# A four-part neighbour search with last-layer units beside it, last layer mostly in whole units

## The chip, the cores and the metric

The kernel runs on one core of one Trainium2 chip. The metric is the device time of one execution in microseconds (us), median of the runs shown. The engines are TensorE (PE), VectorE (DVE), ScalarE (ACT), GpSimd (POOL) and SyncE (SP, which only issues DMAs here); they run independently and meet at semaphores.

## The reference

Four graph layers follow one another over 4096 nodes with 128 features, each with a residual. `adj` is 4096 x 4096 in fp32 and is used in all four:

```python
h = jnp.maximum(_layernorm(x), 0.0); x = x + _L0(h, adj)   # relu([h, adj@h] W + b)
h = jnp.maximum(_layernorm(x), 0.0); x = x + _L1(h, adj)   # normalised (adj+I) h, rows of unit length
h = jnp.maximum(_layernorm(x), 0.0); x = x + _L2(h, adj)   # message and GRU cell
h = jnp.maximum(_layernorm(x), 0.0); x = x + _L3(h, adj)
# _L3(x, A):
z  = leaky_relu(lap_mul(A, x) @ W1 + b1)                  # d * (A @ (d*x)), d = 1/sqrt(row sums of A)
d2 = sq[:, None] + sq[None, :] - 2.0 * (z @ z.T)          # 4096 x 4096 squared distances
S  = exp(-sqrt(max(d2, 0) + 1e-10) / 2)
S  = where(rank of S in its row < 4, S, 0)                # the four nearest nodes of each node
out = lap_mul(S + A, x) @ W2 + b2
```

So the last layer multiplies by `adj` twice: once to get `z`, and, after a search for the four nearest nodes of each row, once more with new row sums.

## The kernel before

`adj` does not fit on the core. It is streamed in units, and two layers share a load where both can use it. A *visit* is one unit of 128 x 2 x 512 numbers (512 KB) that PE multiplies; it is loaded by SP into one of 10 slots of a ring (`load_unit`), which has to wait until PE has used the unit ten visits back. A block is 512 nodes; a block's row of `adj` is 16 units (`UNITS`), numbered `u`, two for each block `kb` of columns. A class `Plan` writes down the order of all 524 visits, which PSUM bank each accumulation has, and after which visit each small step is due on each engine. Layers are numbered `q`; 4 stands for the second multiplication of the last layer.

A unit is multiplied in one of two ways (`visit` in the tensor block):

- *whole*: two fp32 products straight from the ring (the profile shows four matmuls, L441). No other engine is needed. The plan's own cost is 1.73 us (`WHOLE_US`).
- *split*: ACT copies the unit rounded to fp32r (`upper`, `A_hi`), DVE subtracts it from the original (`lower`, L1078, `A_lo`), and PE makes three fp32r products for each half (L436, L437, L438), six matmuls. The plan's cost is 1.38 us (`SPLIT_US`).

The first 396 visits are the first four multiplications. Then come three stages that the change touches.

**The last block and the start of the search.** When the last block of layer 3 is done, PE transposes it (`natural`), DVE makes `z`, PE transposes `z` (L551), ACT squares it, DVE makes the row of squares in three bf16 parts (`square_parts`), PE turns it into a row (`square_row`, L561), ACT writes it into `sq_aug` (`aug_out`).

**The search.** Nodes are taken 128 at a time (a row tile, 32 in all, in the order `seek`). For each, PE fills all eight PSUM banks with scores against all 4096 nodes, in two halves of four banks: four bf16 products with `ones3` (L611) and twelve fp32r products (L613 to L615) per half. ACT moves each half to one of two `scores` buffers (`pair_out`), 2048 columns at a time. DVE finds the eight largest of 4096 (`v_.max`, L1154) and their places (`v_.max_index`, L1156). A `scores` buffer is free when the scan two tiles back is finished. Every four tiles a short chain makes the similarities, the new row sums and the scaled operand of that block: `clamp` (DVE), `similarity` (ACT), `new_degrees` (DVE), `new_roots` (ACT), `new_inverse` (DVE), `scale_last` (ACT, gives `G_last` and its rounded copy), `last_rest` (DVE). POOL stores each scaled block to HBM (L1250). Because the scores have all eight banks, no last-layer visit can run before the last half is moved out.

**The last layer.** 128 visits: the 16 of block 0 whole, then blocks 1 to 7 with two whole units and 14 split ones each, in all 98 split. Beside it POOL gathers the four nearest rows of each node from HBM with indirect DMAs, 128 of them (L1258), once the last block is stored and all scans are done. There are eight landing slots; the gather for tile `t` waits until DVE has weighed tile `t - 8`. ACT scales the four rows (`scale_neighbours`), DVE adds them (`weigh`, L1189, L1191) and after every fourth tile finishes a block (`last_rows`, L1197 to L1205), which SP sends out. After which visit these are placed in the queues of ACT and DVE is set by `LAST_US`, `NEAR_US` and `NEAR_FIRST`:

```python
at = min(UNITS + int((NEAR_FIRST + NEAR_US * t) / LAST_US), UNITS * NB)
self.near_due.setdefault(self.rows_end + at, []).append(t)
```

All queues are in order: a step that waits on ACT holds the `upper` behind it, and so DVE's `lower` and PE.

Of the kernel before, what the change touches and what calls it, by code (L numbers as in the profile page):

```python
# [5 lines left out]
P = 128  # L6
N = 4096
BLK = 512
# [54 lines left out]
WHOLE_BESIDE_SCANS = tuple(range(UNITS))  # L63
WHOLE_LAST = (7, 15)

LAST_US, NEAR_US, NEAR_FIRST = 1.5, 6.1, 9.0


class Plan:


    def __init__(self):
# [25 lines left out]
        for n in range(UNITS * NB):  # L100
            b, j = n // UNITS, n % UNITS
            u = j if b else (NB - 1 - j // HALVES) * HALVES + j % HALVES
            self.visits.append(Visit(len(self.visits), b, u, (4,), j not in (WHOLE_BESIDE_SCANS, WHOLE_LAST)[b > 0]))
            self.spans.setdefault((4, b, 4), [len(self.visits) - 1, 0])[1] = len(self.visits) - 1
# [4 lines left out]
        for t in range(NT):  # L109
            at = min(UNITS + int((NEAR_FIRST + NEAR_US * t) / LAST_US), UNITS * NB)  # L110
            self.near_due.setdefault(self.rows_end + at, []).append(t)
# [12 lines left out]
        for b in range(NB):  # L124
            self.moved["move_out", 4, b] = len(self.moved) + 1

# [74 lines left out]
def gnn_stack(nc, x_in, at_in, pack_in, scaled_rows, out):  # L201
# [4 lines left out]
    with ctx:  # L206
# [18 lines left out]
        a_at, b_at, hi_at = take("area_a", 16), take("area_b", 16), take("area_hi", 4 * STAGED)  # L225

# [23 lines left out]
        colsum = sb("colsum", [P, TPB, BLK])  # L250
# [17 lines left out]
        sq_aug = colsum[0:3, :, :].bitcast(bf16).rearrange("p t (b n) -> p (t b) n", n=BLK)  # L268
        sq_cols = sb("sq_cols", [P, TPB])
        sq_parts = sb("sq_parts", [P, TPB, 3], bf16)  # L270
        sq_rest = sb("sq_rest", [P, 2, TPB])
        ident16 = sb("ident16", [P, P], bf16)
        ones3 = sb("ones3", [3, P], bf16)
# [40 lines left out]
        half_full, half_out, scanned = sem("half_full"), sem("half_out"), sem("scanned")  # L314
# [23 lines left out]

        first_hn = (hn, nat)
# [6 lines left out]
        def _(sp):  # L346
# [15 lines left out]
            sent = 0  # L362
# [9 lines left out]
            for v in PLAN.visits[SLOTS:]:  # L372
                load_unit(v)
                for t in PLAN.near_due.get(v.n - SLOTS - 2, ()):
                    if t % TPB == TPB - 1:
                        send(t // TPB)
                        sent += 1
            for b in range(sent, NB):
                send(b)
# [4 lines left out]
        def _(pe):  # L384
# [17 lines left out]
            def operand_of(v, q, p):  # L402

                kb = v.u // HALVES
                if q == 0 and v.split:
                    pe.wait_ge(firstlo_ready, NB)
                elif q == 0:
                    pe.wait_ge(first_ready, kb + 1)
                elif q < 4:
                    pe.wait_ge(g_ready, nth_h(q - 1, kb) - NB)  # L410
                elif v.b == 0:
                    pe.wait_ge(lastlo_ready if v.split else last_ready, NB - kb)
                else:
                    pe.wait_ge(lastlo_ready, NB)
# [139 lines left out]
            def square_row(b):  # L554
# [5 lines left out]
                for n in range(TPB):  # L560
                    last = mm(ps[0:3, GB, n * P:(n + 1) * P], sq_parts[:, n, :], ident16[:, :], start=True, stop=True)  # L561
# [38 lines left out]


            half_of = lambda c: (c // 4 + 1) % 2
            columns = (*range(4, 8), *range(4))
            bank_of = lambda c: c % 4 + 4 * half_of(c)

            def pair_columns(t, cs):

                at_row = t % TPB * P
                hi, lo = (z[:, t // TPB, at_row:at_row + P] for z in (z_hi, z_lo))
                for c in cs:  # L610
                    mm(ps[:, bank_of(c), :], ones3[:, :], sq_aug[:, c, :], start=True, stop=False)  # L611
                for c in cs:
                    mm(ps[:, bank_of(c), :], hi, z_hi[:, c, :], start=False, stop=False)  # L613
                    mm(ps[:, bank_of(c), :], hi, z_lo[:, c, :], start=False, stop=False)  # L614
                    last = mm(ps[:, bank_of(c), :], lo, z_hi[:, c, :], start=False, stop=True)  # L615
                last.then_inc(half_full, 1)

            def pair_rows(i):
                for half in range(2):
                    pe.wait_ge(half_out, 2 * i + half - 1)  # L620
                    pair_columns(seek[i], columns[4 * half:4 * half + 4])

            def first_pairs(cs):

                for c in cs:
                    pe.wait_ge(aug_ready, nth_in(3, c))
                    pe.wait_ge(zlo_ready, nth_in(3, c))
                pair_columns(seek[0], cs)
# [4 lines left out]
            first_pairs(columns[0:4])  # L633
# [5 lines left out]
            pe.wait_ge(half_out, 2 * NT)  # L639

            for v in PLAN.visits[PLAN.rows_end:]:
                visit(v)
                if v.b and v.u == 2 + (v.b == 1):
# [5 lines left out]
        def _(act):  # L649
# [107 lines left out]
            def aug_out(b):  # L757
                act.wait_ge(sqrow_full, nth_in(3, b))
                f(sq_aug[:, b, :], ps[0:3, GB, :], ACT.Copy).then_inc(aug_ready, 1)
# [74 lines left out]
            def pair_out(i):  # L834
# [3 lines left out]
                for half in range(2):  # L838
                    act.wait_ge(half_full, 2 * i + half + 1)
                    at_col = N // 2 * (1 - half)  # L840
                    f(scores[i % 2][:, at_col:at_col + N // 2],
                      ps[:, 4 * half:4 * half + 4, :].rearrange("p c n -> p (c n)"), ACT.Identity,
                      scale=2.0, bias=neg_sq[:, t:t + 1]).then_inc(half_out, 1)
# [50 lines left out]
            for j, v in enumerate(PLAN.visits[PLAN.rows_end:]):  # L894
                if v.split:
                    upper(v)
                if v.b and j % UNITS == 3:
# [4 lines left out]
            for t in PLAN.near_due.get(PLAN.rows_end + UNITS * NB, ()):  # L902
# [4 lines left out]
        def _(dve):  # L907
# [148 lines left out]
            def square_parts(b):  # L1056
# [6 lines left out]
                half, rest = sq_rest[:, 0, :], sq_rest[:, 1, :]  # L1063
                own.add(v_.tensor_scalar(half, sq_cols[:, :], -0.5, None, ALU.mult))
                own.settle()
                own.add(v_.tensor_copy(sq_parts[:, :, 0], half))
                own.settle()
                own.add(v_.tensor_tensor(rest, half, sq_parts[:, :, 0], ALU.subtract))
                own.settle()
                own.add(v_.tensor_copy(sq_parts[:, :, 1], rest))  # L1070
                own.settle()
                v_.tensor_tensor(sq_parts[:, :, 2], rest, sq_parts[:, :, 1], ALU.subtract).then_inc(sqparts_ready, 1)
# [57 lines left out]
            v_.tensor_copy(ident16[:, :], ident)  # L1130
# [17 lines left out]

            def scan(i):

                t = seek[i]
                dve.wait_ge(half_out, 2 * i + 2)
                row = scores[i % 2][:, :]
                own.add(v_.max(best[:, t, :], row))  # L1154
                own.settle()
                v_.max_index(best_at[:, t, :], best[:, t, :], row).then_inc(scanned, 1)  # L1156
# [50 lines left out]
            for i in range(NT - 2):  # L1207
# [7 lines left out]
                elif i >= TPB:  # L1215
                    last_rest(i // TPB - 1)
            m = NB - 1
# [79 lines left out]
```

## Time and profile before

| | |
|---|---|
| median of 3 runs | 1424.39 us (1424.10 to 1429.17) |
| the profiled execution | 1424.92 us, span in the trace 1423.1 us |
| PE busy | 93% of the span (modelled ends) |
| DVE busy | 84% |
| ACT busy | 56% |
| POOL busy | 12% |
| read from HBM | 286 MB |
| mean granted TensorE clock | 0.977 |

The span is what the trace covers; the device time has 1.8 us more. Times in the text are positions on the trace's own clock, which starts with the span. Busy PE time overlaps itself, as each matmul's end is modelled; the pace of PE is read from the starts of successive matmuls.

### The profile page before, as it was taken

How to read it: one execution, taken by the hardware profiler on the slowest of the kernel's cores; microseconds unless marked ns; L12 is line 12 of the kernel's file. 1: busy time of each engine (PE TensorE's matmuls, PEld its weight loads, DVE VectorE, ACT ScalarE, POOL GpSimd, SP SyncE). 2: the span in 40 equal slices, each digit the busy share in tenths (PEclk: the TensorE clock that was granted, in tenths of full speed). 3: DMA queues.
4: the chain of work that ended last, by engine and by line, in shares of the span. 5: the costliest groups of instructions: out<-in, count | busy, mean ns of one | idle time of the engine just before them, and what ended most of it. 6: DMA issues, size and time to landing. Idle time of an engine off the chain costs nothing.

```text
span 1423.1 us, 15737 instructions
## 1 busy us (share of the span) xinstructions
PE 1321.7 (93%) x5526; PEld 955.9 (67%) x5526; DVE 1191.1 (84%) x1616; ACT 790.9 (56%) x1117; POOL 173.0 (12%) x144
## 2 busy tenths in 40 slices
PE   7999999999899999999999999899989989899983
PEld 4556677788778767777777778555555554677662
DVE  8998889898999878766548998599999998587784
ACT  2423333346766767665557776455555554676773
POOL 0000000000000000000000000000000000888885
PEclk9999999999999999999999999999999999999997
DMA  9787766558676866565558799100000005989993
GB/s 348 230 268 245 223 209 203 181 188 308 235 243 225 280 245 225 181 220 194 179 176 295 264 329 343 55 0 8 8 8 8 8 8 186 371 314 367 377 337 101
DMA packets 82861, 291.49 MB, mean 205 GB/s; under 512 B 10848, under 2 KB 10976, under 8 KB 82784
## 3 DMA queue, kind: packets, MB, share of 16 engines
q1 hardware_dynamic: 78048, 280.01, 56.8%
q0 software_dynamic: 4736, 10.49, 2.5%
q8 instruction: 44, 0.72, 0.2%
q14 instruction: 33, 0.27, 0.1%
HBM read 286.27 MB, written 4.19 MB: 204 GB/s over the span
## 4 chain that ended last, share of the span: by engine, by line
PE 50%; DVE 29%; POOL 12%; issue 6%; ACT 2%; DMA 1%; SPq 0%; POOLq 0%; ACTq 0%; DVEq 0%
POOL landing L1258 12%; PE ps L436 11%; PE ps L438 11%; PE ps L437 11%; DVE best_at L1156 9%; DVE rows_T L1154 9%; PE ps L441 7%; DVE A_lo L1078 6%; PE ps L511 1%; PE ps L539 1%; PE ps L540 1%; PE ps L480 1%; PE ps L474 1%; DVE hn L928 1%; PE ps L498 1%
## 5 line engine op out<-in xcount | busy, mean ns | idle before, releaser
L1078 DVE TENSOR_TENSOR A_lo<-ring,A_hi 128x1024 fp32r<-128x1024 f32 x431 | 508.9, 1219 | 61.7 <-ACT A_hi L651 58.1
L651 ACT ACTIVATE A_hi<-ring 128x1024 fp32r<-128x1024 f32 x431 | 440.0, 1054 | 110.0 <-PE ps L438 98.1
L436 PE MATMUL ps<-A_hi,G_odd_hi 128*128 128x512 f32 x708 | 291.2, 411 | 17.0 <-DVE A_lo L1078 10.1
L438 PE MATMUL ps<-A_hi,G_odd_lo 128*128 128x512 f32 x708 | 280.4, 396 | 0.0
L437 PE MATMUL ps<-A_lo,G_odd_hi 128*128 128x512 f32 x708 | 280.2, 396 | 0.0
L1258 POOL DMA_INDIRECT landing<-scaled_rows,best_at x128 | 166.3, 1299 | 43.4 <-issue 38.7
L436 PEld LDWEIGHTS ps<-A_hi,G_odd_hi 128*128 128x128 f32 x708 | 135.3, 191 | 52.1 <-issue 18.6
L436 PE MATMUL ps<-A_hi,G_even_hi 128*128 128x512 f32 x386 | 162.5, 421 | 0.2 <-DVE A_lo L1078 0.2
L651 ACT ACTIVATE scores<-ps,neg_sq 128x2048 f32<-128x2048 f32 x64 | 124.3, 1963 | 59.9 <-PE ps L615 38.3
L437 PEld LDWEIGHTS ps<-A_lo,G_odd_hi 128*128 128x128 f32 x708 | 135.6, 192 | 29.9 <-issue 3.4
L438 PEld LDWEIGHTS ps<-A_hi,G_odd_lo 128*128 128x128 f32 x708 | 135.6, 192 | 29.8
L1250 POOL DMA_DIRECT2D scaled_rows<-G_last x8 | 6.2, 780 | 1197.5 <-ACT G_last L651 1197.5
L438 PE MATMUL ps<-A_hi,G_even_lo 128*128 128x512 f32 x386 | 150.7, 390 | 0.0
L437 PE MATMUL ps<-A_lo,G_even_hi 128*128 128x512 f32 x386 | 150.4, 390 | 0.0
L1154 DVE MAX8 rows_T<-scores 128x8 f32<-128x4096 f32 x32 | 141.3, 4414 | 9.6 <-ACT scores L651 9.6
L1156 DVE FIND_INDEX8 best_at<-rows_T,scores 128x8 uint32<-128x4096 f32 x32 | 141.4, 4419 | 0.0
L958 DVE TENSOR_TENSOR colsum<-colsum,ring 128x1024 f32<-128x1024 f32 x112 | 133.7, 1219 | 0.0
L441 PE MATMUL ps<-ring,G_first 128*128 128x512 f32 x252 | 113.2, 592 | 0.0
L613 PE MATMUL ps<-z_hi 128*128 128x512 f32 x256 | 110.9, 433 | 0.0
L614 PE MATMUL ps<-z_lo,z_hi 128*128 128x512 f32 x256 | 103.7, 405 | 0.0
L615 PE MATMUL ps<-z_hi,z_lo 128*128 128x512 f32 x256 | 103.7, 405 | 0.0
L611 PE MATMUL ps<-colsum,ones 3*128 3x512 bf16 x256 | 66.9, 380 | 26.8 <-ACT scores L651 26.1
(136 smaller groups left out, 1354.8 us busy)
## 6 DMA issues: line engine op xcount, KB each, us to landing
ring<-adj_t SPq DMA_DIRECT2D x524, 512.0 KB
X<-x_rows SPq DMA_DIRECT2D x8, 256.0 KB, 6.9
scaled_rows<-G_last POOLq DMA_DIRECT2D x8, 256.0 KB, 2.7
landing<-scaled_rows,best_at POOLq DMA_INDIRECT x128
out_rows<-X SPq DMA_DIRECT2D x8, 256.0 KB
pack<-packed SPq DMA_DIRECT2D x1, 836.0 KB, 14.6
pack<-packed SPq DMA_DIRECT2D x1, 192.0 KB, 4.1
```

The source lines that it names most:

```text
L436: mm(acc, G_hi[odd][:, kb, t, :], hi, start=start, stop=False)
L437: mm(acc, G_hi[odd][:, kb, t, :], lo, start=False, stop=False)
L438: done = mm(acc, G_lo[odd][:, kb, t, :], hi, start=False, stop=stop)
L441: done = mm(acc, G[:, kb, t, :], ring[:, s, k, :], start=start, stop=stop)
L613: mm(ps[:, bank_of(c), :], hi, z_hi[:, c, :], start=False, stop=False)
L614: mm(ps[:, bank_of(c), :], hi, z_lo[:, c, :], start=False, stop=False)
L651: return nc.scalar.activation(out_ap, in_ap, func, **k)
L958: ins = v_.tensor_tensor(half, half, ring[:, s, :, :], ALU.add)
L1078: v_.tensor_tensor(A_lo[:, s, :, :], ring[:, s, :, :], A_hi[:, slot_of(v), :, :].bitcast(fp32), ALU.subtract).then_inc(lower_ready, 1)
L1154: own.add(v_.max(best[:, t, :], row))
L1156: v_.max_index(best_at[:, t, :], best[:, t, :], row).then_inc(scanned, 1)
L1258: pool.indirect_dma_start(out=landing[:, k, r, :], out_offset=None, in_=scaled_rows, in_offset=bass.IndirectOffsetOnAxis(ap=best_at[:, t, ...
```

## The change

It does the following.

- `square_parts` makes two fp32r parts in place of three bf16 ones; `square_row` multiplies them in fp32; `sq_aug` is 128 rows deep, cleared once by POOL, and has its own place together with `colsum`. `ones2` replaces `ones3`.
- The search is done in four parts of two banks (`columns`, `pair_columns`, `score_banks`), which rotate through three pairs of banks. Two banks are left. ACT moves 1024 columns at a time (`evicted` counts them).
- 34 last-layer visits are placed into PE's stream before the end of the search: one after each of 17 row tiles from the 9th to the 30th (three tiles in four), and 17 behind the last row tile (11 of blocks 0 and 1, six of block 2). All are whole.
- The remaining 94 visits are whole but for units 4 and 12 of each block (11 visits).
- At the end of the search DVE does both last `max` scans before the first `max_index`, with `clamp` and `new_degrees` between.
- `near_due` counts from the end of the search with 5.2 us for a tile in place of 6.1; SP sends the finished blocks after all loads.

```diff
-WHOLE_BESIDE_SCANS = tuple(range(UNITS))
-WHOLE_LAST = (7, 15)
-LAST_US, NEAR_US, NEAR_FIRST = 1.5, 6.1, 9.0
+LAST_US, NEAR_US, NEAR_FIRST = 1.7, 5.2, 8.0
+SPLIT_EVERY = 8
...
-        for n in range(UNITS * NB):
-            b, j = n // UNITS, n % UNITS
-            u = j if b else (NB - 1 - j // HALVES) * HALVES + j % HALVES
-            self.visits.append(Visit(len(self.visits), b, u, (4,), j not in (WHOLE_BESIDE_SCANS, WHOLE_LAST)[b > 0]))
+        ended = [b * HALVES + half for b in sorted(range(NB), key=lambda b: self.rank[3, b]) for half in range(HALVES)]
+        self.beside = {}
+        for c in range(28):
+            v = self.last_visit(c % 2, ended[c // 2], False)
+            at = 8 + c // 3 * 4 + c % 3
+            self.beside.setdefault(at if at < NT - 2 else NT - 1, []).append(v)
+        for u in ended[:6]:
+            self.beside[NT - 1].append(self.last_visit(2, u, False))
+        self.search_end = len(self.visits)
+        for b in range(2):
+            for u in ended[-HALVES:]:
+                self.last_visit(b, u, False)
+        for b in range(2, NB):
+            for u in range(UNITS):
+                if b > 2 or u not in ended[:6]:
+                    self.last_visit(b, u, u % SPLIT_EVERY == SPLIT_EVERY // 2)
...
+            at = self.search_end + int((NEAR_FIRST + NEAR_US * t) / LAST_US)
+            if t % TPB == TPB - 1:
+                at = max(at, self.search_end + 13, self.spans[4, t // TPB, 4][1] + 8)
+            self.near_due.setdefault(min(at, len(self.visits)), []).append(t)
...
+        columns = [sorted(seek_blocks[2 * q:2 * q + 2]) for q in range(4)]
+        free = [k for k in range(2 * BANKS) if k not in (PLAN.bank[4, 0, 4], PLAN.bank[4, 1, 4])]
+        score_banks = (free[0:2], (AUX, AUX + 1), (TB, GB))
...
+            def pair_columns(i, q):
+                n, at_row = 4 * i + q, seek[i] % TPB * P
+                if n >= len(score_banks):
+                    pe.wait_ge(evicted, n - len(score_banks) + 1)
+                hi, lo = (z[:, seek[i] // TPB, at_row:at_row + P] for z in (z_hi, z_lo))
+                for bank, c in zip(score_banks[n % len(score_banks)], columns[q]):
+                    mm(ps[:, bank, :], ones2[:, :], sq_aug[:, c, :], start=True, stop=False)
+                    mm(ps[:, bank, :], hi, z_hi[:, c, :], start=False, stop=False)
+                    mm(ps[:, bank, :], hi, z_lo[:, c, :], start=False, stop=False)
+                    last = mm(ps[:, bank, :], lo, z_hi[:, c, :], start=False, stop=True)
+                last.then_inc(part_full, 1)
...
+            first_columns(0)
             z_transposes(last_row)
+            first_columns(1)
             square_row(last_row)
-            first_pairs(columns[4:8])
+            first_columns(2)
+            first_columns(3)
             for i in range(1, NT):
-                pair_rows(i)
+                for q in range(4):
+                    pair_columns(i, q)
+                for v in PLAN.beside.get(i, ()):
+                    if v.b == 2:
+                        pe.wait_ge(evicted, 4 * NT)
+                    visit(v)
...
-            scan(NT - 2)
+            scan_values(NT - 2)
+            scan_values(NT - 1)
+            clamp(m)
+            scan_places(NT - 2)
+            new_degrees(m)
+            scan_places(NT - 1)
+            new_inverse(m)
             last_rest(m - 1)
-            scan(NT - 1)
-            clamp(m)
-            new_degrees(m)
-            new_inverse(m)
             last_rest(m)
...
+            pool.wait_ge(u_ready, NB)
+            pool.wait_ge(nat_full, 3 * NB)
+            g.memset(sq_aug[:, :, :].bitcast(fp32), 0.0).then_inc(aug_cleared, 1)
```

## Rows read from the trace of the kernel before

**Rows 1.** The page's costliest groups: line, engine, operation; busy and mean; idle and its releaser.

```profile
L1258 POOL DMA_INDIRECT landing<-scaled_rows,best_at x128 | 166.3, 1299 | 43.4 <-issue 38.7
...
L1154 DVE MAX8 rows_T<-scores 128x8 f32<-128x4096 f32 x32 | 141.3, 4414 | 9.6 <-ACT scores L651 9.6
```

**Rows 2.** Table by stage: window, length, busy of PE, PEld, DVE, ACT, POOL; PEclk, DMA share, GB/s.

```profile
908.00:1181.00 273.00, 246.88 (x976) 155.94 (x975) 271.67 (x125) 150.07 (x127) 4.74 (x6) 0.97 0.02 6
1185.00:1213.00 28.00, 27.54 (x65) 12.27 (x65) 19.58 (x14) 11.30 (x20) 4.50 (x5) 1.00 0.79 274
...
1290.00:1320.00 30.00, 28.04 (x108) 20.63 (x106) 23.17 (x32) 20.89 (x34) 24.82 (x18) 0.94 0.99 363
```

**Rows 3.** Timeline of POOL: start us, us, engine, line; gathers of the last layer.

```profile
1209.38 1.47 POOL L1258 DMA_INDIRECT landing<-scaled_rows,best_at  x1 [4.65 <-DMA scaled_rows<-G_last]
...
1233.41 0.94 POOL L1258 DMA_INDIRECT landing<-scaled_rows,best_at  x1 [0.31 <-issue]
...
1246.01 1.97 POOL L1258 DMA_INDIRECT landing<-scaled_rows,best_at  x1 [0.30 <-issue]
...
1395.52 0.95 POOL L1258 DMA_INDIRECT landing<-scaled_rows,best_at  x1 [0.30 <-issue]
...
1413.42 0.94 POOL L1258 DMA_INDIRECT landing<-scaled_rows,best_at  x1 [0.30 <-issue]
```

**Rows 4.** Timeline of DVE around two of those gathers.

```profile
1228.80 4.63 DVE L1078 TENSOR_TENSOR A_lo<-ring,A_hi 128x1024 fp32r<-128x1024 f32 x4 [0.20 <-issue]
...
1244.80 4.63 DVE L1078 TENSOR_TENSOR A_lo<-ring,A_hi 128x1024 fp32r<-128x1024 f32 x4
```

**Rows 5.** Timeline of PE in the search: the halves of one row tile.

```profile
1175.52 1.03 PE L611 MATMUL ps<-colsum,ones 3*128 3x512 bf16 x4
...
1176.82 0.40 PE L614 MATMUL ps<-z_lo,z_hi 128*128 128x512 f32 x1
...
1178.88 0.39 PE L614 MATMUL ps<-z_lo,z_hi 128*128 128x512 f32 x1
...
1179.43 1.03 PE L611 MATMUL ps<-colsum,ones 3*128 3x512 bf16 x4
```

**Rows 6.** Timeline of PE: the 16 whole units of block 0, then split units.

```profile
1185.46 27.73 PE L441 MATMUL ps<-ring,G_last 128*128 128x512 f32 x64 [2.06 <-ACT scores L651]
1212.63 0.79 PE L436 MATMUL ps<-A_hi,G_odd_hi 128*128 128x512 f32 x1
```

**Rows 7.** Timeline of ACT and DVE at the start of the search.

```profile
906.07 1.97 ACT L651 ACTIVATE scores<-ps,neg_sq 128x2048 f32<-128x2048 f32 x1 [4.47 <-PE ps L615]
...
908.07 4.43 DVE L1154 MAX8 rows_T<-scores 128x8 f32<-128x4096 f32 x1 [9.58 <-ACT scores L651]
```

**Rows 8.** Timelines at the end of the search: the last two scans, the last store.

```profile
1180.33 4.40 DVE L1154 MAX8 rows_T<-scores 128x8 f32<-128x4096 f32 x1
...
1194.29 4.42 DVE L1156 FIND_INDEX8 best_at<-rows_T,scores 128x8 uint32<-128x4096 f32 x1
...
1202.20 0.18 DVE L1175 RECIPROCAL d2inv<-root 128x4 f32<-128x4 f32 x1 [1.15 <-ACT root L651]
...
1203.98 0.75 POOL L1250 DMA_DIRECT2D scaled_rows<-G_last  x1 [16.37 <-ACT G_last L651]
```

**Rows 9.** Two lines asked for by source: their first and last start (us).

```profile
L1035 DVE TENSOR_TENSOR colsum<-colsum x8: 692/693/694, 521.8 to 754.3; 128x512 f32<-128x512 f32 x8
...
L561 PE MATMUL ps<-ident,sq_parts x32: 217/219/311, 789.3 to 898.8; 128*3 128x128 bf16 x32
```

**Rows 10.** Timeline of ACT and DVE at the end of the kernel.

```profile
1400.76 0.60 ACT L651 ACTIVATE rows_T<-ps 128x512 f32<-128x512 f32 x1 [6.44 <-issue]
1401.25 2.44 ACT L651 ACTIVATE landing<-landing,simil 128x128 f32<-128x128 f32 x8
...
1416.00 1.27 ACT L651 ACTIVATE landing<-landing,simil 128x128 f32<-128x128 f32 x4 [3.66 <-DMA landing<-scaled_rows,best_at]
...
1419.99 0.69 DVE L1205 TENSOR_TENSOR X<-X,nat 128x512 f32<-128x512 f32 x1
```

More of the change, by code:

```diff
@@ L360, in send @@
                 sp.dma_start(out[b, :, :, :], X[:, b, :, :]).then_inc(out_stored, 16)
-            sent = 0
             load_x(0)
@@ L373, in _ @@
                 load_unit(v)
[L374 to L378, printed above, removed]
+            for b in range(NB):
                 send(b)
@@ L599, in _, with first_columns @@
                         step(name, p, b)
[L602 to L628, printed above, removed]
+            def pair_columns(i, q):
[9 more added lines that the diff above has]
+                last.then_inc(part_full, 1)
+            def first_columns(q):
+                done = NB if q > 1 else max(nth_in(3, c) for c in columns[q])
+                pe.wait_ge(aug_ready, done)
+                pe.wait_ge(zlo_ready, done)
+                pair_columns(0, q)
             last_row = seek_blocks[-1]
@@ L837, in pair_out @@
                     act.wait_ge(scanned, i - 1)
[L838 to L843, printed above, removed]
+                for q in range(4):
+                    act.wait_ge(part_full, 4 * i + q + 1)
+                    (bank, next_bank), at_col = score_banks[(4 * i + q) % len(score_banks)], columns[q][0] * BLK
+                    f(scores[i % 2][:, at_col:at_col + 2 * BLK], ps[:, bank:next_bank + 1:next_bank - bank, :].rearrange("p c n -> p (c n)"),
+                      ACT.Identity, scale=2.0, bias=neg_sq[:, t:t + 1]).then_inc(evicted, 1)
             def similarity(m):
@@ L893, in _ @@
             scale_last(m)
-            for j, v in enumerate(PLAN.visits[PLAN.rows_end:]):
+            for v in PLAN.visits[PLAN.search_end:]:
                 if v.split:
                     upper(v)
-                if v.b and j % UNITS == 3:
+                if v.n - PLAN.search_end in (6, 10):
+                    move_out(4, (v.n - PLAN.search_end) // 4 - 1)
+                elif v.b > 2 and v.u == 3:
                     move_out(4, v.b - 1)
@@ L901, in _ @@
             move_out(4, NB - 1)
-            for t in PLAN.near_due.get(PLAN.rows_end + UNITS * NB, ()):
+            for t in PLAN.near_due.get(len(PLAN.visits), ()):
                 scale_neighbours(t)
@@ L1147, in _, with scan_values, scan_places @@
                     step(name, p, b)
-            def scan(i):
[L1151 to L1156, printed above, removed]
+            def scan_values(i):
+                dve.wait_ge(evicted, 4 * i + 4)
+                own.add(v_.max(best[:, seek[i], :], scores[i % 2][:, :]))
+            def scan_places(i):
+                own.settle()
+                v_.max_index(best_at[:, seek[i], :], best[:, seek[i], :], scores[i % 2][:, :]).then_inc(scanned, 1)
+            def scan(i):
+                scan_values(i)
+                scan_places(i)
             def clamp(m):
@@ L1231, in _ @@
                         last_rows(t // TPB)
-            for t in PLAN.near_due.get(PLAN.rows_end + UNITS * NB, ()):
+            for t in PLAN.near_due.get(len(PLAN.visits), ()):
                 weigh(t)
```

59 lines of the change are left out of this document (28 added, 31 removed).

## Prediction

> **What bounds the kernel now.** I read the page first, then the table by stage, then the timeline of each engine around the places that the change touches. In the search DVE is the bound: 271.7 of 273 us busy, PE's clock at 0.97, DMA at a share of 0.02 [rows 2]. The first `max` starts at 908.07 [rows 7] and the last `max_index` ends at 1194.29 + 4.42 = 1198.7 [rows 8]: 290.6 us for 32 row tiles, 9.08 each. PE needs 3.91 us for a half [rows 5], 7.8 of the 9.08, and is not used otherwise; the loads stand still.
>
> In the last layer the order turns. Gathers run from 1209.38 to 1413.42, and their idle time is all "issue": POOL never waits for a landing slot [rows 1, 3]. So POOL is busy from end to end, 204.0 us for 127 steps, 1.607 each. PE is done earlier: ACT moves out the last block at 1400.76, and what comes later is the last gathers and their tail [rows 10]. DMA is close to full beside it (share 0.99 at 363 GB/s [rows 2]). Two limits thus lie close together: POOL sets the end, and PE could not end much earlier, since it starts this layer only when the last scores are moved out.
>
> **Why a gather takes 0.94 or 1.97 us.** The one at 1233.41 begins just as a run of `lower` ends (1228.80 + 4.63) and takes 0.94; the one at 1246.01 lies inside the run from 1244.80 to 1249.43 and takes 1.97 [rows 3, 4]. From 1395.52, after the last `lower`, 15 gathers start 17.90/14 = 1.279 us apart [rows 3]. The first 113 steps take 186.1 us, 1.647 each: 41.6 us more than at 1.279, or 0.42 us for each of the 98 split units. The Trainium skill ("SBUF — State Buffer", Who interferes with whom) says that a DVE instruction with two SBUF inputs contends with a GpSimd instruction that reads SBUF; by that, the trace agrees. The same section infers that `tensor_tensor` would not hold up descriptor generation; by that alone gathers would stay as they are, which is the first rival below.
>
> **Before the search.** `square_parts` loses three DVE instructions of some 0.2 us per block; `square_row` goes from bf16 to fp32, four matmuls of 128 columns. A whole unit's fp32 matmul has 512 columns and takes a quarter of 1.70 us (below), so 128 columns cost about 0.1 and the four at most 0.5 us, beside 0.2 now. Over eight blocks that is between -5 and +3 us on engines that have other work beside; I take 0. POOL's clearing of `sq_aug` (4096 elements a row) can start when the last GRU block is made (last L1035 at 754.3) and a transpose later; the first `square_row` is at 789.3 [rows 9]. It has some 30 us. DVE reads 4096 elements in 4.4 us [rows 1]; POOL may take several times that, still hidden. At ten times, ACT would wait about 15 us with `upper` behind it, part of which DVE and the ring could not give back. I take 0.
>
> At the start of the search PE now puts 8 matmuls, not 16, ahead of the transposes of the last `z`: 8 at 0.229 us (2.06 us for nine [rows 5]), 1.8 us. Three small DVE steps less: 0.6. The last move-out before the first scan is of 1024 columns, not 2048: half of 1.97, so 1.0 [rows 7]. Sum -3.4 us (bounds 0, if PE's second 8 matmuls take the place of the first, and -4.5). The first scan starts at 904.7.
>
> **The search.** DVE's work per tile is unchanged, so 9.08 stands if PE keeps up. A tile is 32 matmuls of 0.229, `ones2` priced like its fp32r neighbours: 7.33 us. Whole units: 16 took 1212.63 - 1185.46 = 27.17 us, 1.70 each, and the next matmul 0.4 more for the change of type [rows 6]. Beside scores I take 1.75, at most 2.1. Three visits in four tiles: (4 x 7.33 + 3 x 1.75)/4 = 8.64 us of 9.08, at the clock of 0.97 8.91, and at 2.1 still 8.9 before the clock. A tile's scores are due a whole scan after their buffer is free, and four move-outs of 1.0 us and a part of 1.8 us need under 6 us, so a late part has 3 us of slack. I take 0; at most the missing 0.2 us x 22 tiles, 4 us. All of DVE's other work stays. So 17 units of 1.7 us disappear under the scans.
>
> **The end of the search.** The last buffer is free at 1180.33 - 3.4 = 1176.9 [rows 8]. The first move-out frees a pair at 1177.9, PE's last part is done at 1179.8. From there it goes on without waiting: 17 whole units, 28.9 us, to 1208.7. The block scaled last is needed only behind them.
>
> DVE does max, max, index, index, the same 18.4 us, to 1195.3; but `clamp` and `new_degrees` lie inside, and `new_inverse` follows at once, where it came 3.5 us after the scan (1202.20 against 1198.7). The store came 1.8 us after it, the first gather 5.4 us later [rows 3, 8]: now 1197.2 and 1202.6, 6.8 us earlier than before.
>
> **The last layer on PE.** 83 whole units at 1.70, 141.1; 11 split at the plan's 1.38, 15.2; seven transposed blocks at 0.7 (estimate, under the 1.03 of four matmuls in [rows 5]), 4.9. From 1208.7 to 1369.9. The clock: 1.00 over the whole units, 0.94 in a later window [rows 2]. Two such windows of 30 us cost 3.4 us; none and all are 0 and 11. I take 3.4: 1373.3. Before, PE had this work spread up to 1400.6, with 32 us less in price but 17 units more to do and the loads and `lower` to wait for.
>
> **The gathers.** 127 x 1.279 + 11 x 0.42 = 167.0 us after 1202.6: the last starts at 1369.6. Before, ACT took it up 2.58 us later [rows 3, 10]: 1372.2. The last `scale_neighbours` stand behind the last `move_out` in ACT's queue, so PE's end decides by some 3 us. If only the gathers counted, the end would be 1369.6 + 9.7 (1423.1 - 1413.42) = 1379.3.
>
> **The tail.** ACT starts 0.15 after PE, the scalings 0.49 later and take 2.44; from the end of the last scaling (1417.27) to the end of the span it was 5.8 [rows 10]. 1373.3 + 3.1 + 5.8 = 1382.2. Sending all blocks after the loads costs nothing: seven of them go while the ring is already loaded.
>
> **The loads.** From 1177 on 101 units of 0.524 MB and 128 gathers of 0.066 MB are 61.4 MB. At PE's pace this is 308 + 50 = 358 GB/s against 363 seen [rows 2], tight, but ten slots give 17 us of slack; DMA decides only under 61.4/196 = 313 GB/s on the mean.
>
> Waits added in queues: `scale_neighbours(t)` waits on ACT before an `upper`. Gather t is landed at about 1202.6 + 5.3(t + 1) + 2.5, the visit behind it due at 1208.7 + 1.7(8 + 5.2t)/1.7: ACT is 8 us ahead at t = 0, and about 5 at t = 27, before the last split unit. No hold. Sum: span 1382.2; the profiled execution had 1.8 us beside its span (1424.9 against 1423.1) and is 0.5 us from the median, so 1384.
>
> **Rivals.**
> - *The gathers do not get faster.* If the load of the DMA engines, not `lower`, makes them long, the step stays 1.607: 1202.6 + 204.1 + 9.7 = 1416.4, and 1418 with the 1.8. That is -0.45%, no change that can be told. For it: DMA is idle too after 1395. Against: the 0.94 at 1233.41. Chance 0.06.
> - *They get half as fast as I say,* since `weigh` and `last_rows`, now bunched, or the loads lengthen them too: 1.45 gives 1202.6 + 184.2 + 9.7 + 1.8 = 1398, and ACT then holds the uppers. 0.10.
> - *DMA is the bound,* 330 GB/s beside the gathers: 1.87 us a unit, 16 us more less some slack: 1393 to 1400. 0.05.
> - *The clock falls (slower).* PE is now busy 95% of the search and all of the last layer, and nothing covers it. With clock c it costs 22 (8.64/c - 9.08) + 190 (1/c - 1) us. At 0.885 this eats the 40 us won; at 0.85 the time is about 1438. Against: 0.97 to 1.00 in all windows with PE at work but the last ones at 0.94 [rows 2]. 0.04.
> - *My sum,* 1376 to 1392: 0.75.
>
> **Numbers.** 1384, range 1376 to 1402, which holds the sum and the two middle rivals; low end by no clock loss (-3.4) and -4 before the search. 0.5% (7 us) is about what a measurement tells from no change. Faster 0.90, same 0.06, slower 0.04.
>
> **What would show it.** Gathers start near 1203 and 1.3 us apart, 0.94 but beside `lower`; first scan near 905 and 9.1 us a tile, with DVE never waiting for scores; PE starts whole units near 1180, 1.70 us apart, to about 1373; POOL ends a few us before. Wrong if DVE waits for ACT's scores, if gathers last over 1.2 us with DVE idle, if PE waits for the ring, or if PEclk is under 0.95.

## The result, and the profile after

| | before | after |
|---|---|---|
| median | 1424.64 us (1424.10 to 1429.17, 4 runs) | 1380.76 us (1379.87 to 1382.12, 4 runs) |
| profiled execution, its span | 1424.92, 1423.1 | 1379.87, 1378.0 |
| PE, DVE, ACT, POOL busy | 93, 84, 56, 12% | 96, 79, 52, 10% |
| mean granted clock | 0.977 | 0.996 |

The ratio is 0.9686 with a 95% interval of 0.9664 to 0.9708: 44 us, 3.1%, less. 1384 was forecast, with 1376 to 1402 as the range.

Two of the page's costliest groups, after, against [rows 1]. The scan's `max` takes what it took; the 128 gathers take 990 ns on the mean where they took 1299.

```profile
L1167 DVE MAX8 rows_T<-scores 128x8 f32<-128x4096 f32 x32 | 141.3, 4415 | 7.4 <-ACT scores L672 7.4
...
L1287 POOL DMA_INDIRECT landing<-scaled_rows,best_at x128 | 126.7, 990 | 43.5 <-issue 38.1
```

The table by stage, after (columns as in [rows 2]): the search, the stretch from its last scores to the first gathers, and the rest of the last layer.

```profile
900.00:1176.00 276.00, 261.85 (x1057) 198.75 (x1056) 271.34 (x125) 164.15 (x189) 4.75 (x6) 0.99 0.12 39
1180.00:1209.00 29.00, 29.00 (x69) 12.93 (x68) 15.04 (x12) 7.43 (x16) 7.29 (x9) 1.00 0.85 292
1209.00:1370.00 161.00, 160.31 (x426) 77.84 (x425) 52.74 (x113) 53.48 (x140) 120.95 (x122) 1.00 0.95 344
```

In the search DVE is as full as it was, and DMA is no longer idle. Behind it PE is busy 160.3 of 161 us at a clock of 1.00; from 1290 to 1320 us the kernel before had 0.94 [rows 2].

The timeline of POOL, after, against [rows 3, 8]: the last store, the first gather, two from the middle, the last.

```profile
1195.86 0.75 POOL L1279 DMA_DIRECT2D scaled_rows<-G_last  x1 [13.21 <-ACT G_last L672]
...
1201.38 1.02 POOL L1287 DMA_INDIRECT landing<-scaled_rows,best_at  x1 [4.78 <-DMA scaled_rows<-G_last]
...
1235.50 1.22 POOL L1287 DMA_INDIRECT landing<-scaled_rows,best_at  x1 [0.30 <-issue]
...
1245.85 1.57 POOL L1287 DMA_INDIRECT landing<-scaled_rows,best_at  x1 [0.31 <-issue]
...
1365.91 0.94 POOL L1287 DMA_INDIRECT landing<-scaled_rows,best_at  x1 [0.30 <-issue]
```

127 steps in 164.5 us are 1.296 each, against 1.607.

The timeline of DVE, after, against [rows 7, 8]: the first scan, and the last `max` and `max_index`.

```profile
903.39 4.43 DVE L1167 MAX8 rows_T<-scores 128x8 f32<-128x4096 f32 x1 [6.96 <-ACT scores L672]
...
1180.47 4.43 DVE L1167 MAX8 rows_T<-scores 128x8 f32<-128x4096 f32 x1 [0.41 <-ACT scores L672]
...
1189.76 4.42 DVE L1171 FIND_INDEX8 best_at<-rows_T,scores 128x8 uint32<-128x4096 f32 x1
```

The scans last from 903.39 to 1194.18, 9.09 us a tile. DVE waited for scores twice: before the first scan, and 0.41 us before the last `max`.

The timeline of PE, after, against [rows 5, 6]: one last-layer visit beside the scores, and the 19 whole visits that follow the last scores without a gap.

```profile
1042.43 1.88 PE L462 MATMUL ps<-ring,G_last 128*128 128x512 f32 x4
1043.74 0.79 PE L630 MATMUL ps<-sq_aug,ones 128*128 128x512 f32 x1
...
1179.55 32.78 PE L462 MATMUL ps<-ring,G_last 128*128 128x512 f32 x76
```

The end of the kernel, after, against [rows 10], on ACT:

```profile
1369.28 0.60 ACT L672 ACTIVATE rows_T<-ps 128x512 f32<-128x512 f32 x1 [6.80 <-PE ps L462]
1369.77 2.43 ACT L672 ACTIVATE landing<-landing,simil 128x128 f32<-128x128 f32 x8
```

Before, ACT had moved out the last block at 1400.76 and got the last gather's rows at 1416.00. Now the last gather starts at 1365.91, and 3.4 us later ACT takes PE's last block, and behind it the last two tiles' scalings with no wait for rows. By the 2.58 us of before, these rows were there at 1368.5, 1.3 us before ACT came to them: PE sets the end, with POOL close behind it. The span is 45.1 us shorter: the last move-out comes 31.5 us earlier, and what follows it takes 8.8 us in place of 22.4, since no gather is awaited there any more.

### The profile page after: what moved, and what is told of

Same layout as the page of the kernel before. It is cut to its first block, busy times and chain, and to the rows that moved or that the text cites. A ratio compares the mean times of both kernels' runs of the same rounds, so it can differ in the third digit from the quotient of the medians.

```text
span 1378.0 us, 15241 instructions
## 1 busy us (share of the span) xinstructions
PE 1325.3 (96%) x5384; PEld 949.2 (69%) x5384; DVE 1089.8 (79%) x1504; ACT 721.2 (52%) x1094; POOL 137.2 (10%) x146
## 4 chain that ended last, share of the span: by engine, by line
PE 66%; DVE 29%; ACT 2%; issue 2%; DMA 1%; SPq 0%; ACTq 0%; DVEq 0%
PE ps L462 19%; PE ps L457 12%; PE ps L459 12%; PE ps L458 12%; DVE best_at L1171 9%; DVE rows_T L1167 9%; DVE A_lo L1095 5%; PE ps L532 1%; PE ps L560 1%; PE ps L561 1%; PE ps L495 1%; PE ps L501 1%; DVE hn L951 1%; PE ps L519 1%; DVE stats L936 1%
## 5 line engine op out<-in xcount | busy, mean ns | idle before, releaser
L1095 DVE TENSOR_TENSOR A_lo<-ring,A_hi 128x1024 fp32r<-128x1024 f32 x344 | 409.6, 1220 | 64.9 <-ACT A_hi L672 62.6
L672 ACT ACTIVATE A_hi<-ring 128x1024 fp32r<-128x1024 f32 x344 | 354.8, 1056 | 106.3 <-PE ps L459 92.2
L457 PE MATMUL ps<-A_hi,G_odd_hi 128*128 128x512 f32 x534 | 217.8, 408 | 2.1 <-DVE A_lo L1095 2.1
L459 PE MATMUL ps<-A_hi,G_odd_lo 128*128 128x512 f32 x534 | 209.1, 392 | 0.0
L458 PE MATMUL ps<-A_lo,G_odd_hi 128*128 128x512 f32 x534 | 208.4, 390 | 0.0
L462 PE MATMUL ps<-ring,G_last 128*128 128x512 f32 x468 | 205.7, 592 | 0.0
L672 ACT ACTIVATE scores<-ps,neg_sq 128x1024 f32<-128x1024 f32 x128 | 137.4, 1111 | 51.3 <-PE ps L633 39.5
L462 PEld LDWEIGHTS ps<-ring,G_last 128*128 128x128 f32 x468 | 88.4, 190 | 99.4 <-issue 97.5
L1287 POOL DMA_INDIRECT landing<-scaled_rows,best_at x128 | 126.7, 990 | 43.5 <-issue 38.1
L630 PE MATMUL ps<-sq_aug,ones 128*128 128x512 f32 x256 | 109.0, 426 | 14.8 <-ACT scores L672 14.1
L458 PEld LDWEIGHTS ps<-A_lo,G_odd_hi 128*128 128x128 f32 x534 | 100.7, 189 | 22.4 <-issue 3.1
```

The lines of the kernel that those rows point to most:

```text
L457: mm(acc, G_hi[odd][:, kb, t, :], hi, start=start, stop=False)
L458: mm(acc, G_hi[odd][:, kb, t, :], lo, start=False, stop=False)
L459: done = mm(acc, G_lo[odd][:, kb, t, :], hi, start=False, stop=stop)
L462: done = mm(acc, G[:, kb, t, :], ring[:, s, k, :], start=start, stop=stop)
L630: mm(ps[:, bank, :], ones2[:, :], sq_aug[:, c, :], start=True, stop=False)
L672: return nc.scalar.activation(out_ap, in_ap, func, **k)
```

## The experiments

The kernels ran in groups, each on one chip together with the kernel before, and their ratios are against it there. The changed kernel, unaltered, was in two of the groups. In the one with the order of scans and the two with a visit after every row tile it took 1379.98 us (1378.48 to 1382.19), ratio 0.9678 [0.9660, 0.9696]. In the one with the split, behind and paced kernels it took 1379.96 (1379.19 to 1380.55), 0.9681 [0.9663, 0.9698]. The kernel before with a whole last layer ran on another chip, without the changed kernel beside it. The "stretch" of which some expectations speak is told under "Three runs with a stretch of their own".

> The changed kernel unaltered, timed beside the next three: 1381 us.

> The changed kernel unaltered, beside a repetition of three edits whose traces had a stretch of some 30 to 40 us from about 1233 in which PE issued one matmul in 2 to 3 us, ACT and DVE stood, SP issued hardly a load and only POOL's gathers went on. If that stretch belongs to the chip those three shared, this kernel has it too whenever the three have it, and none has it elsewhere (1381 us here); if it belongs to their programs, they have it here and this one doesn't.

### Most of the last layer split again

```diff
-                    self.last_visit(b, u, u % SPLIT_EVERY == SPLIT_EVERY // 2)
+                    self.last_visit(b, u, u % SPLIT_EVERY != SPLIT_EVERY - 1)
```

> 14 of 16 last-layer units split again. Without the stretch: DVE's subtractions lengthen the gathers again, the last starts near 1397, time 1409 us; PE alone as the bound would give 1377. With the stretch: 1403 to 1417 again.

Measured: 1404.63 us (1402.73 to 1407.15), ratio 0.9856 [0.9837, 0.9875]; 24.7 us more than the changed kernel beside it. The gathers of this kernel, by source (shortest, median and longest ns; first and last start):

```profile
L1287 POOL DMA_INDIRECT landing<-scaled_rows,best_at x128: 940/948/1982, 1202.1 to 1393.3; - x128
```

The step is 191.2/127 = 1.506 us, and (1.506 - 1.296) x 127 / 68 = 0.39 us more for each split unit, against the 0.42 read from the trace of before. The timelines of POOL and DVE show the mechanism, around 1233 and around 1299 us:

```profile
1233.38 1.55 POOL L1287 DMA_INDIRECT landing<-scaled_rows,best_at  x1 [0.30 <-issue]
1235.23 1.97 POOL L1287 DMA_INDIRECT landing<-scaled_rows,best_at  x1 [0.30 <-issue]
...
1298.19 0.94 POOL L1287 DMA_INDIRECT landing<-scaled_rows,best_at  x1 [0.30 <-issue]
1299.44 1.98 POOL L1287 DMA_INDIRECT landing<-scaled_rows,best_at  x1 [0.30 <-issue]
```

```profile
1232.90 3.49 DVE L1095 TENSOR_TENSOR A_lo<-ring,A_hi 128x1024 fp32r<-128x1024 f32 x3
...
1298.24 3.60 DVE L1095 TENSOR_TENSOR A_lo<-ring,A_hi 128x1024 fp32r<-128x1024 f32 x3 [0.20 <-ACT A_hi L672]
```

It is not any overlap that counts, but a `lower` that is running when the gather starts. The gather at 1298.19 starts 0.05 us before the first `lower` of the run and takes 0.94, though it lies beside it; the one at 1299.44 starts with the second one running and takes 1.98. In this trace 39 gathers start while a `lower` is running that has at least 0.2 us to go, and every one takes what that `lower` has left plus 0.82 us: 1.55 with 0.74 to go, 1.97 with 1.15. The 52 such gathers of the kernel before and the nine of the changed one do the same; over all hundred it is 0.81 to 0.83 us. So the gather is held until the `lower` has ended. Nine gathers of the split version start within 0.01 us of a `lower` or up to 0.4 us ahead of one, with no other DVE instruction running, and take 0.94 or 0.95. ACT's `upper`, which comes with every split unit too, is not the cause: 26 gathers lie beside an `upper` and no `lower`, with a median of 0.94 and none above 1.07.

The Trainium skill ("SBUF — State Buffer", Who interferes with whom) infers that `tensor_tensor` would not hold up descriptor generation. By that alone the gathers would stay as they are, and the trace does not agree: 1.97 against 0.94 us, and the step grows with the number of `lower`. Whether the descriptors or POOL's reading of the indices is held up, no trace here tells.

PE has 68 x 0.32 = 22 us less priced work in this kernel and still waits. Its waits from 1205 us on:

```profile
PE ps L457 <- DVE A_lo L1095: 32.0, 12, 4.8
PE ps L495 <- ACT rows_T L672: 0.7, 1, 0.7
```

These waits go back to the gathers as well. Eleven of the 12 are longer than 0.5 us, and ahead of ten of these the last thing that ACT waited for before the `upper` was the landing of gathered rows; then this `upper` was late, then DVE's `lower`, then PE. So the time does not show PE's work, and both limits end together: PE's last block is moved out at 1393.88, and ACT then waits 0.23 us for the rows of the last gather:

```profile
1395.88 1.28 ACT L672 ACTIVATE landing<-landing,simil 128x128 f32<-128x128 f32 x4 [0.23 <-DMA landing<-scaled_rows,best_at]
```

### The kernel before with a whole last layer

This leaves the search, its eight banks and the start of the last layer as before. Which units are split, and the pace of 5.2 us a tile, are the changed kernel's; the first step stays at 9.0 us, where the changed kernel has 8.0. The running maximum in the edit keeps the near steps (the scaling and weighing of a tile's four rows) in the order of the tiles.

```diff
-            ... j not in (WHOLE_BESIDE_SCANS, WHOLE_LAST)[b > 0]))
+            ... b > 0 and j % 8 == 4))
-LAST_US, NEAR_US, NEAR_FIRST = 1.5, 6.1, 9.0
+LAST_US, NEAR_US, NEAR_FIRST = 1.7, 5.2, 9.0
...
+        at = 0
         for t in range(NT):
-            at = min(UNITS + int((NEAR_FIRST + NEAR_US * t) / LAST_US), UNITS * NB)
+            at = max(at, UNITS + int((NEAR_FIRST + NEAR_US * t) / LAST_US))
+            if t % TPB == TPB - 1:
+                at = max(at, self.spans[4, t // TPB, 4][1] - self.rows_end + 8)
+            at = min(at, UNITS * NB)
```

> The kernel before, with its search as it was, but the last layer in whole units but two of each block (14 split), and the gathers' steps placed as in the changed kernel. Theory: the gathers are short (127 x 1.28 + 14 x 0.42 = 168 us, last start near 1378), and PE sets the end: 1212.6 + 98 x 1.70 + 14 x 1.38 + 4.9 = 1403.4, and 8.9 us of tail and 1.8 beside the span make 1414 us, so only a quarter of the whole gain. Rival (whole units alone bring the gain, the search in four parts little): about 1381 to 1390 us.

Measured: 1415.04 us (1414.69 to 1416.85), ratio 0.9939 [0.9920, 0.9958]. The gathers, by source:

```profile
L1262 POOL DMA_INDIRECT landing<-scaled_rows,best_at x128: 940/944/1995, 1209.9 to 1377.6; - x128
```

The gathers alone lose 36 us of their end (1413.4 to 1377.6), and the kernel gains 10: PE, now some 28 us behind them, transposes its last block at 1406.4. Cheaper gathers do not pay unless PE's work gets shorter too.

### All 34 early visits behind the search

```diff
-            self.beside.setdefault(at if at < NT - 2 else NT - 1, []).append(v)
+            self.beside.setdefault(NT - 1, []).append(v)
```

> The 17 visits between the row tiles behind the search again. Without the stretch: PE has 28.9 us more to do behind the search and the time is 1410 us. With it: 1443 us or more again.

Measured: 1409.68 us (1407.49 to 1410.92), ratio 0.9887 [0.9869, 0.9905]; 29.7 us more than the changed kernel, for 17 visits, against 17 x 1.70 = 28.9. The last gather starts at 1368.5, as good as unmoved, and PE's last block is transposed at 1400.3. In the search the window by engines reads:

```profile
900.00:1170.00 270.00, 238.56 (x970) 188.17 (x970) 263.85 (x121) 162.45 (x187) 4.75 (x6) 0.96 0.02 6
```

The scans take as long with the visits (9.09 us a tile) as without them.

### The old pace of the near steps

```diff
-LAST_US, NEAR_US, NEAR_FIRST = 1.7, 5.2, 8.0
+LAST_US, NEAR_US, NEAR_FIRST = 1.7, 6.1, 9.0
```

> The gathers' steps placed 6.1 us a tile apart again. If the stretch belongs to the chip of the first look: 1387 us, for five tiles more that are scaled and weighed after PE's end, and no such stretch. If it belongs to the program: 1425 us or more again.

Measured: 1386.32 us (1386.11 to 1387.34), ratio 0.9726 [0.9709, 0.9744]; 6.4 us more than the changed kernel beside it. Its timeline of ACT at the end:

```profile
1370.31 0.60 ACT L672 ACTIVATE rows_T<-ps 128x512 f32<-128x512 f32 x1 [14.93 <-PE ps L462]
1370.81 8.27 ACT L672 ACTIVATE landing<-landing,simil 128x128 f32<-128x128 f32 x28
```

The last block is moved out 0.5 us later than in the changed kernel beside it (1369.85). But 28 scalings, seven tiles, are placed behind it in ACT's queue where the changed kernel has eight: 8.27 against 2.43 us. ACT was idle for 14.93 us just before, though the rows of the first of these tiles had landed. The last gather starts 4.2 us later too (1370.33 against 1366.15), though POOL waited for no slot; its rows, landed near 1372.9, are not awaited, as ACT's scalings last to 1379.1. Here the pace costs on the tail.

### The old order of the last two scans

```diff
-            scan_values(NT - 2)
-            scan_values(NT - 1)
-            clamp(m)
-            scan_places(NT - 2)
-            new_degrees(m)
-            scan_places(NT - 1)
-            new_inverse(m)
-            last_rest(m - 1)
-            last_rest(m)
+            scan(NT - 2)
+            last_rest(m - 1)
+            scan(NT - 1)
+            clamp(m)
+            new_degrees(m)
+            new_inverse(m)
+            last_rest(m)
```

> The changed kernel with the two last scans in the old order (max, places, max, places, and clamp and new_degrees only behind them). Theory: the last store and the gathers come 3.5 us later (first near 1204.9, last near 1369.4); ACT could take up the last tile at 1372.0, where it did so at 1370.9, so the time grows by only 1 us, to 1382. Rival (the gathers set the end one for one): 1384.5.

Measured: 1380.72 us (1379.62 to 1383.48), ratio 0.9678 [0.9662, 0.9694], the same as the changed kernel's beside it. The timeline of POOL, the last store, the first gather and the last:

```profile
1199.83 0.75 POOL L1277 DMA_DIRECT2D scaled_rows<-G_last  x1 [16.69 <-ACT G_last L672]
...
1205.29 1.02 POOL L1285 DMA_INDIRECT landing<-scaled_rows,best_at  x1 [4.71 <-DMA scaled_rows<-G_last]
...
1372.08 0.94 POOL L1285 DMA_INDIRECT landing<-scaled_rows,best_at  x1 [0.30 <-issue]
```

The store and the first gather come 3.9 and 4.0 us later than in the changed kernel beside it (1195.96 and 1201.32), about the 3.5 of the theory: this is what the new order gives to the gathers. The profiled execution was the slowest of the five, 1383.48 us. In it the gathers also take longer, 1.313 us a step, the last one starts at 1372.08 and not at 1369.4, and ACT waits 1.24 us for its rows behind the last block. So the old order uses up POOL's slack, and in that execution more than that; on the median of five the end does not move by more than can be told.

### A visit after every row tile, 22 in place of 17

```diff
-            at = 8 + c // 3 * 4 + c % 3
+            at = 8 + c
```

> The changed kernel with a visit after every row tile from the 9th to the 30th, 22 in place of 17. PE then needs 7.43 + 1.72 = 9.15 us a tile against 9.08 of DVE. Theory: the search grows by no more than 2 us, PE ends 8.5 - 2 us earlier, and now the gathers set the end, about 2.4 us earlier than now at most: 1378 to 1380. Rival (PE, with no slack, makes the scans wait for scores by more than it saves): 1383 or more.

Measured: 1379.89 us (1379.32 to 1381.97), ratio 0.9676 [0.9660, 0.9693]: no gain, though the scans did not get longer. The timelines of PE and then ACT of this kernel from 1211 to 1221 us show where it went.

```profile
1211.42 2.31 PE L462 MATMUL ps<-ring,G_last 128*128 128x512 f32 x5
1220.00 0.77 PE L457 MATMUL ps<-A_hi,G_odd_hi 128*128 128x512 f32 x1 [6.26 <-DVE A_lo L1095]
1220.56 0.63 PE L458 MATMUL ps<-A_lo,G_odd_hi 128*128 128x512 f32 x1
1220.99 0.63 PE L459 MATMUL ps<-A_hi,G_odd_lo 128*128 128x512 f32 x1
```

```profile
1212.62 0.57 ACT L672 ACTIVATE rows_T<-ps 128x512 f32<-128x512 f32 x1
1216.37 1.28 ACT L672 ACTIVATE landing<-landing,simil 128x128 f32<-128x128 f32 x4 [3.17 <-DMA landing<-scaled_rows,best_at]
1217.55 1.04 ACT L672 ACTIVATE A_hi<-ring 128x1024 fp32r<-128x1024 f32 x1
```

PE comes to its first split unit earlier, but the `upper` of this unit stands in ACT's queue behind the scalings of a tile whose gathers have not landed. PE idles 6.26 us, and then runs for a while at the lower clock level: its matmuls start 0.43 us apart instead of 0.23. Its last block is moved out at 1369.33, as in the changed kernel (1369.28). The gathers would have left little more: the last starts at 1366.9, and with the 9.7 us from there to the end of the span and the 1.8 beside it, as in the kernel before, that is an estimate of 1378.4.

### The same, and no unit split

```diff
-            at = 8 + c // 3 * 4 + c % 3
+            at = 8 + c
...
-                    self.last_visit(b, u, u % SPLIT_EVERY == SPLIT_EVERY // 2)
+                    self.last_visit(b, u, False)
```

> As the one with a visit after every row tile, and no split unit in the last layer. Theory: PE +3.5 us for 11 units more in whole form, the gathers -11 x 0.42 = -4.6 us; both limits then lie near 1371 to 1374 on the trace: 1375 to 1377. Rival: the gathers are at their floor already (1.25 us each wherever the split units go), nothing gained over the 1378 to 1380 of the other.

Measured: 1375.84 us (1375.04 to 1378.12), ratio 0.9650 [0.9633, 0.9667], the best of the versions: 4.1 us less than the changed kernel beside it, and the two ranges do not meet. Its gathers:

```profile
L1287 POOL DMA_INDIRECT landing<-scaled_rows,best_at x128: 940/945/1405, 1201.8 to 1362.6; - x128
```

The step is 160.8/127 = 1.266, and PE waits for no `A_lo` any more. The longest gathers, up to 1.41 us without any `lower`, start beside other DVE additions of two SBUF tiles; one of `weigh`, as POOL and then DVE show it:

```profile
1252.29 1.19 POOL L1287 DMA_INDIRECT landing<-scaled_rows,best_at  x1 [0.30 <-issue]
```

```profile
1252.23 0.42 DVE L1208 TENSOR_TENSOR landing<-landing 128x256 f32<-128x256 f32 x1 [1.07 <-ACT landing L672]
```

Over the 128 gathers this comes to some 2 us (160.8 against 127 x 1.25). Five visits more hidden are 8.5 us, 11 units whole instead of split cost 11 x 0.32 = 3.5 us: 5.0 by the prices. PE sets the end, and the last gather starts 2.4 us before the last move-out (1362.56 and 1364.97).

### Three runs with a stretch of their own

The split, behind and paced kernels had first run on another chip, the same programs, with these results: 1415.71 us (1403.40 to 1416.94), 1449.00 (1442.99 to 1453.21) and 1429.55 (1424.70 to 1439.10), ratios 0.9894 [0.9842, 0.9946], 1.0156 [1.0113, 1.0199] and 1.0033 [1.0011, 1.0055].

> The changed kernel with 14 of 16 last-layer units split as before (79 split visits behind the search in place of 11). Theory (DVE's subtractions lengthen the gathers, about 0.42 us for each split unit): the gathers take 127 x 1.28 + 79 x 0.42 = 196 us from about 1201.4, the last starts near 1397, POOL sets the end again, and the time is 1409 us; gathers of 1.97 us come back. Rival (the gathers became short because the loads are spread otherwise, and PE is what counts): PE's work falls from 162 to 140 us, the gathers stay at 1.30 us, and the time is about 1377 us. Also open: PE's granted clock fell to 0.94 in windows of the kernel before's last layer and was 1.00 in the changed one's; if the split units are the cause, windows at 0.94 come back here.

> The changed kernel, but the 17 visits that stood between row tiles now stand behind the last row tile with the other 17. Theory (the visits between the scans cost nothing there, and PE sets the end): PE has 17 x 1.70 = 28.9 us more to do behind the search, everything else stays, 1410 us. Rival (the visits slow the scans, or DMA traffic beside them does): the first scan to the last takes less than the 290 us of the changed kernel, and the time is some us under 1410.

> The changed kernel with the gathers' steps placed 6.1 us a tile apart and 9.0 from the start, as before, in place of 5.2 and 8.0. Theory: the gathers themselves don't change (POOL finds its slot free), but seven tiles in place of two are scaled and weighed behind PE's last move-out, five times 1.25 us on ACT: 1387 us. Rival 1: no difference (1381), because the end hangs on PE alone. Rival 2: POOL waits for slots and the last gather starts 5 us or more later, 1392 us or more.

They were 11, 39 and 43 us over what the same programs took on the second chip. The traces of all three have one stretch in which most of the core stands, beginning between 1224 and 1235 us and lasting from some 22 us (behind) to some 45 (split). It is not in every execution: of the split kernel's four, one took 1403.40 us, what it took on the second chip. For the paced kernel, the window and two of its waits (the releaser is given as "remote"):

```profile
1230.00:1260.00 30.00, 12.38 (x20) 3.93 (x18) 0.00 (x0) 0.00 (x0) 22.66 (x24) 0.63 0.31 90
```

```profile
ACT rows_T L672 <- remote: 43.5, 1, 43.5
DVE nat L1216 <- remote: 32.7, 1, 32.7
```

PE's matmuls start 2.8 us apart, DVE and ACT do nothing, DMA moves 90 GB/s, and POOL's gathers go on as always, 24 in 30 us. (In the other two DVE and ACT do a little, and POOL pauses too.) The changed kernel on the second chip has in the same window:

```profile
1230.00:1260.00 30.00, 30.00 (x83) 14.78 (x82) 10.00 (x22) 10.26 (x27) 22.99 (x24) 1.00 0.99 353
```

The kernel before, on the first chip, took its usual 1426.81 us (1421.48 to 1428.61). The changed kernel itself was not run there. So the stretch depends on the chip or the occasion and is not shown to depend on the program; what it is stays open, and no conclusion above rests on these three runs.

## Why the prediction was right, point by point

- **What sets the end.** Before, POOL did; after, PE ends the chain and the last gather ran 3.4 us ahead of the last move-out, forecast as "some 3". The two limits moved together, as the runs with one of them alone show: whole units without hidden visits gave 10 us (before's search) and 16 us (the new search, 1425.54 - 1409.68), and the hidden visits the other 29.7. PE's own work is no shorter by the prices: 30 whole units and 98 split ones were 186 us, 100 whole and 11 split are 185. Its end came 31.5 us earlier since it starts some 6 us earlier and no longer waits: 186 us of work and 5 of transposes had taken it from 1185.5 to 1400.6.
- **Start of the search.** Forecast 904.7, measured 903.39; 4.7 us gained and not 3.4. The last scores' matmuls start 1.6 us earlier where 2.4 was forecast, and the smaller move-out gives 0.9 where 1.0 was. The other 2.2 were not in the term: at the old start 16 matmuls took 6.2 us, most of them 0.42 apart, at a granted clock of 0.63 from 896 to 903 us; now 16 take 3.8 us, at a clock of 1.00. The clearing on POOL took 3.5 us from 761.2, long before the first `square_row` at 789.4. `square_row` itself takes 0.9 us for the last block, over the bound of 0.5: the product in fp32 shows eight matmuls 0.11 apart, not four. `square_parts` was not measured alone.
- **The search.** 9.09 us a tile as forecast. A visit with the change of type takes 1.31 + 0.4 = 1.7 us of PE (1.75 taken), the scores' matmuls are 0.232 apart (0.229), a move-out of 1024 columns takes 1.11 us (1.0). DVE waited 0.4 us in all for scores once it had begun, where "never" was forecast.
- **The end of the search.** Last store 1195.86 (1197.2), first gather 1201.38 (1202.6): both are early by the 1.3 us of the start. The new order of scans brings 4 us of it, as its own run shows (first gather at 1205.29 with the old order, 1201.32 beside it); the time hardly feels it, since PE sets the end.
- **The gathers.** 1.296 us a step against 1.315. The term that was a little too large is the free step: 1.279 came from the tail of the old trace; the free step here is 0.94 + 0.30 = 1.25 us. The main rival (gathers long from DMA load) fell: 0.94 us at a DMA share of 0.99. So did the middle one: what `weigh` and `last_rows` add is some 2 us over all gathers, as the version without split units shows, and not 17.
- **PE in the last layer.** 100 whole, 11 split, seven transposes are 190.1 us by the prices, and 1179.55 to 1369.1 is 189.5. The mis-sized term is the clock: 3.4 us were taken for lows after the model of 0.94 in the old trace, and none came. PE's last product was due at 1373.3 and came at 1369.1; these 4.2 us are the whole difference between the span forecast, 1382.2, and the span measured, 1378.0. (The "32 us less in price" that the prediction gives the kernel before is 28 by its own prices, 87 x 0.32; nothing was summed from it.)
- **Waits added in queues.** "No hold" came true: PE waited for no `A_lo`. The margin was thin: with five visits more hidden, one `upper` behind a tile's scalings cost PE 6.3 us.
- **The tail** took 8.9 us from PE's last product to the end of the span, as forecast, and 1.8 lie beside the span.
- **DMA** moved 353 GB/s at a share of 0.99 with PE busy 30.00 of 30 us (the window from 1230 us above). It did not decide.
- **The clock as the slower rival** fell the other way: with more PE work the mean clock is 0.996, against 0.977.

## What to carry to other kernels

When two engines end close together, price both after the change: here whole units alone were worth 10 to 16 us, hidden visits with split units 21 (1425.54 - 1404.63), and both together 45. A pass that a scan on another engine bounds is room for whole units of later work, if the banks for it can be freed; but a step that waits for a transfer must not stand in an in-order queue ahead of one that feeds the critical engine (6.3 us in one place). And the choice between a cheap product that needs two helpers and a dearer one that needs none is to be priced with what the helpers hold up: the 0.32 us that a split unit saved PE cost 0.39 us of gathers.

## What the runs showed of the hardware

- **PE's clock was lower where PE waited, not where it had more to do.** In the last layer the changed kernel makes PE wait once, for 0.7 us, and the granted clock is 1.00 throughout. The split version, with 12 waits of up to 4.8 us for `A_lo`, has 0.91 from 1209 to 1390 us and 0.88 for the first window below. Split units alone are not the cause: in the second window, of the kernel before, PE has split units and a few transposes, is busy 28.95 of 30 us, and has 1.00. In the search the clock is 0.99 with 17 visits put into PE's pauses, and 0.94 to 0.97 in the three kernels without them. No run varied the waits alone, so this is what goes together and not a cause shown. The split version's window, and that of the kernel before:

```profile
1233.00:1261.00 28.00, 22.31 (x84) 16.98 (x85) 21.92 (x31) 18.79 (x34) 22.52 (x19) 0.88 0.88 315
```

```profile
850.00:880.00 30.00, 28.95 (x136) 23.14 (x135) 27.50 (x39) 24.45 (x33) 0.00 (x0) 1.00 0.96 350
```

- **A gather costs POOL 0.94 us and the next starts 0.30 later,** at a DMA share of 0.99 as behind the last load. When a `lower` is running as it starts, it takes what is left of it plus 0.82 us, up to 1.99; beside a shorter addition of two SBUF tiles up to 1.41; and it stays at 0.94 when the `lower` starts just after it.
- **Most of a core can stand for some 22 to 45 us,** in three programs on one chip, and not in the same programs on another. Without its repetition beside the changed kernel, the paced version (1429.55 against the 1426.81 of the kernel before) would have read as the loss of the whole gain.
